# A new step table for five engines, and the output projection issued in halves instead of quarters

## The reference

```
h = exp(delta * A) * h + delta * Bm * xc        # per channel (1024) and state (16), over 8192 steps
y = sum over states of h * Cm  +  xc * D
x1 = x + ga * ((y * silu(z)) @ W_out.T)
```

## Time and profile before

| | us |
|---|---|
| median of 3 runs (5697.18 to 5701.3) | 5697.24 |
| the profiled execution, its own time | 5697.24 |
| its span, first to last instruction | 5695.4 |
| of it, chunk by chunk (from the first `times_b` of chunk 0 at 171.4 to that of chunk 15 at 3640.9), 15 chunks | 3469.5 |
| the chunk whose first `times_b` starts at 3179.88, to the next one's at 3410.47 | 230.6 |

### The profile page before, as it was taken

One profiled execution on the slowest core, in us unless ns is written; L12 is line 12 of the kernel. 1 busy time (PEld: TensorE's weight loads), 2 busy tenths in 40 slices (PEclk: granted clock), 3 DMA queues, 4 the chain that ended last, 5 costly groups with the idle time before them and its releaser, 6 DMA issues. The chain is left out here.

```text
span 5695.4 us, 76622 instructions
## 1 busy us (share of the span) xinstructions
PE 4878.5 (86%) x21894; PEld 3374.1 (59%) x21894; DVE 4986.4 (88%) x4382; ACT 3044.8 (53%) x6526; POOL 4001.5 (70%) x1946
## 2 busy tenths in 40 slices
...
GB/s 101 143 179 178 172 193 170 175 185 166 188 171 181 191 154 192 173 173 194 167 175 180 171 189 171 176 163 68 34 34 33 28 33 33 29 31 33 29 31 26
DMA packets 394604, 728.33 MB, mean 128 GB/s; under 512 B 44051, under 2 KB 44179, under 8 KB 394102
## 3 DMA queue, kind: packets, MB, share of 16 engines
...
## 5 line engine op out<-in xcount | busy, mean ns | idle before, releaser
L551 POOL TENSOR_TENSOR slot<-du,b_row 128x1024 f32<-128x1024 f32 x1024 | 2404.3, 2376 | 48.6 <-PE y_ps L914 43.8
L806 DVE TENSOR_TENSOR_SCAN decay<-decay,state,slot 128x1024 f32<-128x1024 f32 x592 | 1389.2, 2347 | 52.0 <-ACT slot L723 50.6
L714 ACT ACTIVATE decay<-delta,rate 128x512 f32<-128x512 f32 x2048 | 1326.2, 679 | 33.4 <-issue 10.6
L914 PEld LDWEIGHTS y_ps<-ident,slot 128*128 128x128 f32 x8192 | 1009.0, 150 | 334.9 <-issue 215.6
L914 PE MATMUL y_ps<-ident,slot 128*128 128x128 f32 x8192 | 1098.2, 287 | 89.0 <-POOL slot L558 83.7
L558 POOL TENSOR_TENSOR slot<-slot,c_row 128x1024 f32<-128x1024 f32 x432 | 1024.6, 2372 | 76.4 <-ACT state L703 74.0
L806 DVE TENSOR_TENSOR_SCAN slot<-decay,state,slot 128x1024 f32<-128x1024 f32 x432 | 1011.9, 2342 | 72.2 <-ACT slot L723 70.3
L1266 POOL TENSOR_TENSOR hq<-hid,qinv 128x1408 f32<-128x1408 f32 x64 | 166.4, 2600 | 1238.3 <-DVE qinv L1293 1238.3
L856 PE MATMUL work_ps<-h_t,win 128*128 128x512 f32 x2048 | 995.0, 631 | 36.0 <-DVE delta L777 19.6
L812 DVE TENSOR_TENSOR slot<-decay,c_row 128x1024 f32<-128x1024 f32 x592 | 724.3, 1224 | 56.1 <-DVE decay L806 3.2
L1234 ACT ACTIVATE act_gate<-gate_ps 128x512 f32<-128x512 f32 (+1 forms) x192 | 108.2, 564 | 1119.6 <-PE gate_ps L1375 621.5
...
## 6 DMA issues: line engine op xcount, KB each, us to landing
b_row<-b_c_rows SPq DMA_DIRECT2D x1024, 256.0 KB, 3.8
c_row<-b_c_rows SPq DMA_DIRECT2D x1024, 256.0 KB, 3.7
...
```

The lines of the kernel that those rows point to most:

```text
L551: pool.tensor_tensor(slot[:, u % SLOTS, :, :], du[:, p % 2, :, :], two(b_row[:, u % BC_RING, :]), ALU.mult).then_inc(S["ub_ready"], 1)
L714: act.activation(decay[u % 2][:, i, :], delta[:, p % 2, i, :], ACT.Exp, scale=rate[:, 2 * p + i, n:n + 1]).then_inc(S["decay_ready"], 1)
L806: dve.tensor_tensor_scan(d if u in DVE_C else h, d, h, state[:, 2 * p, n:n + 1], ALU.mult, ALU.add).then_inc(S["scan_done"], 1)
L914: op = pe.matmul(y_ps[i][:, s, :], slot[:, u % SLOTS, i, s * P:(s + 1) * P], ident[:, :], is_transpose=True, start=False, stop=(n == N - 1 ...
```

## The change

PARTS = 4 goes: a block of the output projection (8 products of 512 columns) is issued as two steps of 4 products instead of four steps of 2. All tables that say at which position a step is issued are replaced (PE, ACT, DVE, POOL, SP), and BANK is replaced. The steps themselves, their number apart from the projection's, the list DVE_C, the slots and the lags stay. Cut to its core (of ACT, DVE and SP the middle positions are left out; SP's loads and stores of the same transfers move too):

```diff
-PARTS = 4
...
 BANK = {
-    ("c", 0): 0, ("c", 1): 0, ("c", 2): 0, ("c", 3): 0, ("c", 4): 0, ("c", 5): 0, ("c", 6): 1, ("c", 7): 1,
+    ("c", 0): 0, ("c", 1): 0, ("c", 2): 0, ("c", 3): 0, ("c", 4): 0, ("c", 5): 0, ("c", 6): 0, ("c", 7): 0,
     ("d", 0): 1, ("d", 1): 1, ("d", 2): 1, ("d", 3): 1, ("d", 4): 1, ("d", 5): 1, ("d", 6): 1, ("d", 7): 1,
-    ("h", 0): 0, ("h", 1): 0, ("h", 2): 0, ("h", 3): 0, ("i", 0): 0, ("i", 1): 0, ("i", 2): 0, ("i", 3): 0,
-    ("i", 4): 0, ("i", 5): 1, ("i", 6): 1, ("i", 7): 0, ("o", 0): 0, ("o", 1): 0, ("o", 2): 1, ("o", 3): 1,
-    ("x", 0): 1, ("y", 0): 0, ("y", 1): 1, ("y", 2): 0, ("y", 3): 0, ("y", 4): 0, ("y", 5): 1, ("y", 6): 0,
-    ("y", 7): 0, ("z", 0): 0, ("z", 1): 0, ("z", 2): 0, ("z", 3): 0, ("z", 4): 0, ("z", 5): 0, ("z", 6): 1,
+    ("h", 0): 0, ("h", 1): 0, ("h", 2): 1, ("h", 3): 1, ("i", 0): 0, ("i", 1): 1, ("i", 2): 0, ("i", 3): 0,
+    ("i", 4): 1, ("i", 5): 0, ("i", 6): 1, ("i", 7): 1, ("o", 0): 0, ("o", 1): 0, ("o", 2): 0, ("o", 3): 1,
+    ("x", 0): 1, ("y", 0): 0, ("y", 1): 0, ("y", 2): 0, ("y", 3): 1, ("y", 4): 0, ("y", 5): 1, ("y", 6): 1,
+    ("y", 7): 0, ("z", 0): 1, ("z", 1): 0, ("z", 2): 0, ("z", 3): 0, ("z", 4): 0, ("z", 5): 0, ("z", 6): 0,
     ("z", 7): 0,
 }
 
 PE_STEPS = {
-    0: [("d", 3, 0), ("z", 5, 0)], 3: [("y", 6, -1)], 6: [("y", 7, -1)], 8: [("z", 6, 0)], 9: [("o", (0, 0), -1)],
-    10: [("o", (0, 1), -1)], 11: [("o", (0, 2), -1)], 12: [("o", (0, 3), -1)], 13: [("d", 4, 0)], 14: [("z", 7, 0)],
-    15: [("o", (1, 0), -1)], 16: [("o", (1, 1), -1), ("d", 5, 0)], 17: [("o", (1, 2), -1)],
-    18: [("o", (1, 3), -1), ("h", 1, 1)], 20: [("y", 0, 0), ("o", (2, 0), -1)], 21: [("o", (2, 1), -1)],
-    22: [("o", (2, 2), -1)], 23: [("o", (2, 3), -1), ("h", 3, 1)], 24: [("h", 0, 1), ("o", (3, 0), -1)],
-    25: [("o", (3, 1), -1), ("h", 2, 1)], 26: [("o", (3, 2), -1), ("i", 0, 1)], 27: [("o", (3, 3), -1), ("c", 0, 1)],
-    28: [("i", 1, 1), ("y", 1, 0)], 32: [("i", 2, 1)], 33: [("d", 6, 0)], 34: [("c", 1, 1)],
-    35: [("c", 2, 1), ("i", 3, 1), ("d", 7, 0)], 36: [("i", 4, 1)], 39: [("c", 3, 1)],
-    40: [("c", 4, 1), ("i", 5, 1), ("y", 2, 0)], 42: [("c", 5, 1), ("i", 6, 1)], 43: [("y", 3, 0)], 46: [("c", 6, 1)],
-    49: [("i", 7, 1)], 50: [("c", 7, 1)], 51: [("z", 0, 1)], 53: [("x", 0, 1)], 54: [("d", 0, 1), ("z", 1, 1)],
-    55: [("d", 1, 1)], 57: [("z", 2, 1), ("y", 4, 0)], 59: [("y", 5, 0)], 61: [("z", 3, 1)],
-    63: [("d", 2, 1), ("z", 4, 1)],
+    1: [("z", 5, 0)], 3: [("y", 6, -1)], 4: [("d", 3, 0), ("y", 7, -1)], 5: [("z", 6, 0)], 7: [("o", (0, 0), -1)],
+    8: [("o", (0, 1), -1)], 9: [("z", 7, 0), ("o", (1, 0), -1)], 10: [("o", (1, 1), -1)],
+    13: [("h", 2, 1), ("h", 3, 1)], 14: [("d", 4, 0), ("o", (2, 0), -1)], 15: [("o", (2, 1), -1)], 16: [("h", 1, 1)],
+    18: [("o", (3, 0), -1)], 19: [("o", (3, 1), -1)], 20: [("d", 5, 0)], 22: [("h", 0, 1)], 23: [("i", 0, 1)],
+    24: [("c", 0, 1)], 26: [("y", 0, 0)], 27: [("i", 1, 1)], 28: [("i", 2, 1)],
+    29: [("c", 1, 1), ("d", 6, 0), ("y", 1, 0)], 33: [("c", 2, 1)], 34: [("i", 3, 1)],
+    36: [("c", 3, 1), ("i", 4, 1), ("y", 2, 0)], 37: [("d", 7, 0)], 38: [("c", 4, 1)], 40: [("i", 5, 1)],
+    43: [("i", 6, 1)], 44: [("c", 5, 1)], 45: [("i", 7, 1)], 46: [("y", 3, 0)], 47: [("c", 6, 1)], 48: [("z", 0, 1)],
+    50: [("c", 7, 1)], 52: [("y", 4, 0)], 53: [("z", 1, 1), ("y", 5, 0)], 54: [("x", 0, 1)],
+    55: [("d", 0, 1), ("z", 2, 1)], 56: [("d", 1, 1)], 57: [("z", 3, 1)], 59: [("d", 2, 1)], 62: [("z", 4, 1)],
 }
 ACT_STEPS = {
-    0: [("sp_exp", 2, 0)], 1: [("sp_ln", 2, 0)], 3: [("z_out", 4, 0), ("xd", 0, 0)], 5: [("sp_exp", 3, 0)],
-    6: [("y_out", 6, -1), ("y_out", 7, -1)], 7: [("z_out", 5, 0)], 8: [("sp_ln", 3, 0), ("xd", 3, 0)],
-    10: [("lead", 1, 0)], 12: [("xd", 2, 0)], 13: [("z_out", 6, 0)], 14: [("seed", 0, 1)], 15: [("sp_exp", 4, 0)],
-    16: [("sp_ln", 4, 0), ("z_out", 7, 0)],
-    17: [("ln_apply", 0, 1), ("ln_apply", 1, 1), ("ln_apply", 2, 1), ("ln_apply", 3, 1)], 18: [("sp_exp", 5, 0)],
...
-    50: [("in_out", 7, 1), ("y_out", 4, 0), ("y_out", 5, 0)], 52: [("conv_out", 7, 1), ("silu_x", 0, 1)],
-    53: [("z_out", 0, 1)], 55: [("x_out", 0, 1)], 57: [("sp_exp", 0, 1), ("xd", 1, 1)], 58: [("sp_ln", 0, 1)],
-    59: [("z_out", 1, 1)], 60: [("sp_exp", 1, 1)], 61: [("sp_ln", 1, 1), ("z_out", 2, 1)], 62: [("lead", 0, 1)],
-    63: [("z_out", 3, 1)],
+    0: [("sp_exp", 2, 0)], 1: [("z_out", 4, 0)], 2: [("sp_ln", 2, 0)], 3: [("y_out", 7, -1)], 4: [("z_out", 5, 0)],
+    5: [("y_out", 6, -1)], 7: [("seed", 0, 1), ("sp_exp", 3, 0)], 8: [("ln_apply", 0, 1), ("z_out", 6, 0)],
+    10: [("ln_apply", 1, 1)], 11: [("sp_ln", 3, 0)], 12: [("z_out", 7, 0)],
+    13: [("ln_apply", 2, 1), ("ln_apply", 3, 1), ("lead", 1, 0), ("xd", 2, 0)], 14: [("h_out", 2, 1), ("h_out", 3, 1)],
+    15: [("sp_exp", 4, 0)], 17: [("sp_ln", 4, 0)], 18: [("y_out", 0, 0), ("y_out", 1, 0)], 19: [("xd", 3, 0)],
+    20: [("xd", 5, 0)], 21: [("h_out", 1, 1), ("sp_exp", 5, 0)], 22: [("h_out", 0, 1)],
...
+    49: [("conv_out", 6, 1)], 50: [("z_out", 0, 1), ("y_out", 4, 0), ("y_out", 5, 0)], 51: [("conv_out", 7, 1)],
+    52: [("silu_x", 0, 1)], 54: [("z_out", 1, 1)], 55: [("xd", 1, 1)], 56: [("x_out", 0, 1)], 57: [("sp_exp", 0, 1)],
+    58: [("sp_ln", 0, 1), ("z_out", 2, 1)], 60: [("sp_exp", 1, 1), ("xd", 0, 1)], 62: [("sp_ln", 1, 1)],
+    63: [("z_out", 3, 1), ("lead", 0, 1)],
 }
 DVE_STEPS = {
-    (0, 1): [("sp_sum", 2, 0)], (1, 1): [("sp_diff", 2, 0)], (2, 1): [("sp_out", 2, 0)], (5, 0): [("ln_stats", 0, 1)],
-    (7, 0): [("sp_sum", 3, 0)], (8, 0): [("sp_diff", 3, 0), ("gate", 6, -1)], (8, 1): [("sp_out", 3, 0)],
-    (9, 0): [("gate", 7, -1)], (10, 0): [("ln_stats", 1, 1), ("ln_stats", 2, 1), ("ln_stats", 3, 1)],
-    (10, 1): [("ln_mean", 0, 1)], (13, 1): [("residual", 0, -1)], (14, 1): [("sp_sum", 4, 0)],
-    (15, 0): [("sp_diff", 4, 0)], (16, 0): [("sp_out", 4, 0)], (18, 1): [("sp_sum", 5, 0), ("residual", 1, -1)],
-    (19, 0): [("sp_diff", 5, 0)], (19, 1): [("sp_out", 5, 0)], (21, 1): [("gate", 0, 0)],
-    (22, 0): [("residual", 2, -1)], (27, 0): [("residual", 3, -1)],
-    (27, 1): [("x1_stats", 0, -1), ("x1_stats", 2, -1)], (31, 1): [("gate", 1, 0)], (33, 1): [("sp_sum", 6, 0)],
...
-    (43, 1): [("x1_stats", 3, -1)], (46, 1): [("x1_stats", 1, -1)], (47, 0): [("gate", 3, 0)],
-    (55, 1): [("x_low", 0, 1)], (57, 1): [("sp_sum", 0, 1)], (58, 0): [("sp_diff", 0, 1)], (58, 1): [("sp_out", 0, 1)],
-    (59, 1): [("sp_sum", 1, 1)], (60, 0): [("sp_diff", 1, 1)], (60, 1): [("sp_out", 1, 1), ("gate", 4, 0)],
-    (62, 1): [("gate", 5, 0)],
+    (0, 1): [("ln_stats", 0, 1), ("ln_stats", 1, 1), ("sp_sum", 2, 0)], (3, 1): [("ln_stats", 2, 1)],
+    (4, 0): [("ln_stats", 3, 1), ("sp_diff", 2, 0)], (4, 1): [("ln_mean", 0, 1), ("sp_out", 2, 0)],
+    (5, 1): [("gate", 6, -1)], (6, 0): [("gate", 7, -1)], (9, 0): [("sp_sum", 3, 0)], (9, 1): [("residual", 0, -1)],
+    (10, 1): [("sp_diff", 3, 0)], (11, 1): [("sp_out", 3, 0)], (13, 1): [("residual", 1, -1)],
+    (15, 0): [("sp_sum", 4, 0), ("residual", 2, -1)], (16, 1): [("sp_diff", 4, 0)], (18, 0): [("sp_out", 4, 0)],
+    (20, 0): [("residual", 3, -1)], (22, 0): [("sp_sum", 5, 0)], (24, 0): [("sp_diff", 5, 0)],
+    (25, 1): [("sp_out", 5, 0), ("x1_stats", 2, -1)], (26, 1): [("gate", 0, 0)], (31, 0): [("sp_sum", 6, 0)],
...
+    (41, 1): [("sp_out", 7, 0)], (42, 1): [("x1_stats", 1, -1)], (43, 1): [("x1_stats", 3, -1)],
+    (46, 1): [("gate", 3, 0)], (51, 1): [("gate", 4, 0)], (52, 1): [("gate", 5, 0)], (56, 0): [("x_low", 0, 1)],
+    (57, 1): [("sp_sum", 0, 1)], (58, 0): [("sp_diff", 0, 1)], (58, 1): [("sp_out", 0, 1)],
+    (60, 0): [("sp_sum", 1, 1)], (61, 0): [("sp_diff", 1, 1)], (61, 1): [("sp_out", 1, 1)],
 }
 POOL_STEPS = {
-    10: [("du", 1, 0)], 15: [("lead_mul", 1, 0)], 16: [("newton", 0, 1)], 23: [("du", 2, 0)], 28: [("lead_mul", 2, 0)],
-    43: [("du", 3, 0)], 44: [("lead_mul", 3, 0)], 62: [("du", 0, 1)], 63: [("lead_mul", 0, 1)],
+    7: [("newton", 0, 1)], 13: [("du", 1, 0)], 15: [("lead_mul", 1, 0)], 28: [("du", 2, 0)], 31: [("lead_mul", 2, 0)],
+    44: [("du", 3, 0)], 47: [("lead_mul", 3, 0)], 63: [("du", 0, 1), ("lead_mul", 0, 1)],
 }
...
                     def proj_mm(arg, c):
-                        s, part = arg
+                        s, half = arg
                         b = BANK["o", s]
-                        if part == 0:
+                        if half == 0:
                             if BANK["o", s] != BANK["y", NB - 1]:
                                 wait(pe, *piece_read("y", NB - 1, c))
                             take("o", s, c)
-                        for j in range(part * NB // PARTS, (part + 1) * NB // PARTS):
+                        for j in range(half * NB // 2, (half + 1) * NB // 2):
                             op = pe.matmul(work_ps[b][:, :], xc[c.parity][:, j, s * P:(s + 1) * P], wout[:, j, :],
                                            start=(j == 0), stop=(j == NB - 1))
```

(8 more changed lines are left out.)

24 lines of the change are left out of this document (15 added, 9 removed).

## The result

| | before | after |
|---|---|---|
| median of 4 runs each, side by side (us) | 5699.04 | 5845.17 (5841.19 to 5854.15) |
| ratio, 95% interval | | 1.0256 (1.0244 to 1.0270) |
| span of the profiled execution | 5695.4 | 5843.8 |
| from the first `times_b` of chunk 0 to that of chunk 15, divided by 15 | 231.3 | 240.9 |
| the same without chunk 0, whose body has no projection, divided by 14 | 231.7 | 241.9 |

A forecast was written before the change was run, and what follows sets the result against it. POOL was taken to pace each chunk, so only its waits count: 8.0 lost early less 3.2 saved late is +4.8, taken as 4.6; 15 x 4.6 = 69 on 5697.2 gives 5766 us, 1.2% slower, range 5690 to 5820.

The forecast's parts named there:

- what paces a chunk: POOL paces a 230.6 us chunk; its operations stay, so only its 7.0 us of waits and added waits can move.
- rival "same": The two parts cancel, or POOL's work alone decides: 5697 us; chance 0.09.
- the early part's mechanism: Positions 0 to 29: late projection blocks hold DVE at residuals, so POOL waits 9.1 us instead of 1.1; 8.0 lost a chunk.
- the walk: Working the new order through one chunk, t = 0 at its first `times_b`, each step starting when engine and inputs are ready.
- the weakest step: PE's time at `z 6`, which waits for `gate 7` (27.9); 4 us there would turn the sign.
- the faster rival: Early waits are absorbed and stay at 1.1; only the late 3.2 us gain is left: 5649 us; chance 0.15.
- The step that failed first: `residual 3`, DVE position 20, reached at 83.4, waits for block 3 to 86.7; `times_c` of unit 19 waits 1.8 us.
- the late part's gain: Positions 52 to 63: POOL's waits fall from 6.0 to 2.8 us a chunk, 3.2 saved.
- The early part of before: POOL's early wait in the old kernel, taken as 1.1 us at position 6 of one chunk.
- The loop's end: The few us that every second chunk adds there were left as they are.
- The middle: Positions 30 to 51: ACT waits 1 to 2 us, but where POOL has no `times_c` soon, so 0.
- SP queue: B rows behind moved loads or stores are hidden, so no cost; without that cover up to 4.8 us a chunk.

The follow-up runs named there:

- e4: Changed kernel with 2 of the 8 products of each projection block, the other 6 left out; 5646.94 us in one run.
- e8: Changed kernel with block 3 of the projection in bank 0 at its old PE positions, h 1 behind it; 5798.36 us, ratio 1.0173.
- e1: Changed kernel with one swap, y 5 issued ahead of z 1 at PE position 53; 5819.56 us, ratio 1.0217.
- e5: Kernel before with 2 of the 8 products of each projection block, the others left out; 5675.38 us in one run.
- e9: Kernel before with d 1 moved from PE position 55 to 57, and d 3 and z 5 from 0 to 2; 5646.5 us, ratio 0.9906.
- e2: Changed kernel with block 3 in bank 0 and two PE positions earlier, ahead of h 1, residual 3 at DVE position 19; 5810.14 us, ratio 1.0200.
- e10: Changed kernel with POOL's lead_mul 0 moved from position 63 to position 0 of the next body; 5858.72 us, ratio 1.0278.

## Why the prediction was wrong in size

**Right: what paces a chunk.** POOL's work stayed at 222.9 us a chunk, and the time moved with its waits alone. The rival "same", by which POOL's work alone decides, is refuted: ranked by occupancy the engines look alike in the two kernels, and the time differs by 2.6%.

**Right: the early part's mechanism, with the walk's own numbers.** `z 6`, the weakest step, was walked to t = 27.9, and starts at 29.5 in the chunk shown (3089.28 less 3059.78). The walk had `residual 0` wait 2.2 and be served at 41.6, the trace has 2.44 and 42.8 (3102.60 less 3059.78); `residual 2` 3.9 and 68.0, the trace 3.75 and 69.7. The chunk shown begins behind the loop's pause; in bodies without it the two come at 41.9 and 68.8. POOL's waits at 12, 17 and 19 were walked as 0.9, 1.4 and 3.3 and are 1.3, 1.9 and 3.4 in the mean. That PE would be earlier and absorb them, the faster rival, did not come; e4 shows what less work of PE would have given.

**The step that failed first: `residual 3`, "reached at 83.4", waiting for block 3 "to 86.7", and POOL's 1.8 us behind it.** It was reached at 85.3 and waited to 91.5; POOL waited 4.5 in the mean. That the bank holds block 3 was in the walk ("where `d` and `xd` hold it"); that the half behind this wait runs slowly was not: its half is 3.43 us there, and took 6.57. Of the 4.8 us by which block 3 ends late, 1.7 are there already at `residual 2`, and 3.0 are the slow half. The prediction had used this very effect for `z 2` in the late part, from the row of 5.25 us after a wait, and left it out here, where it is behind a wait of 6.88 us, the second longest of PE in the chunk. This term was 2.7 us a chunk too small, of which the slow half is 2.4 by the estimate above. All early waits together (12.9 in the mean for 9.1) were 3.8 too small. e8 confirms the place: without the collision 3.1 us a chunk come back.

**The second: the late part's gain.** It was to be 6.0 to 2.8. It is 5.0 to 4.2. After: the walk put `y 5` ahead of `z 1` at PE 53 (its text does not print this step), and the table says the reverse; `gate 5` then holds DVE, and POOL waits 2.7 at 55 instead of 1.6. e1 makes that swap and gives 1.4 us a chunk. This is an error of reading, not of the chip. Before: the wait at 62 is 2.25 in the chunk that I chose and 1.4 in the mean, so one chunk was not typical there.

**An error that went the other way.** The early part of before was put at 1.1 us from one chunk. In the mean it is 2.0 (0.4 at 3, 1.6 at 6), so 0.9 us less was lost. The chunk was called typical by its sum, 7.0 for 8; its positions were not.

**The loop's end, left "as they are", cost little more than before.** The row `POOL slot <- issue` suggests otherwise: 18.9 us for 4.8, 3.6 to 4.0 each in five bodies for 0.8 to 1.1. But before, the same pause reaches POOL through ACT. In one such body (POOL, then ACT):

```profile
2018.96 2.37 POOL L551 TENSOR_TENSOR slot<-du,b_row 128x1024 f32<-128x1024 f32 x1 [1.08 <-issue]
2022.99 2.35 POOL L558 TENSOR_TENSOR slot<-slot,c_row 128x1024 f32<-128x1024 f32 x1 [1.66 <-ACT state L703]
```

```profile
2022.63 0.21 ACT L703 ACTIVATE state<-slot 128x2 f32<-128x2 f32 x1 [3.40 <-issue]
```

With that wait at the first `times_c` the pause costs POOL 1.07 us a body before and 1.35 after, over the 14 bodies. The `lead` that POOL waits 0.42 for at 63 is in the late part's 4.2, as it is in the forecast's 2.8. The ledger for a body with a projection, the forecast's 8.0 - 3.2 = 4.8 as the start:

| correction, us a chunk | |
|---|---|
| early waits after, 12.9 for 9.1 (of it 2.7 at position 21) | +3.8 |
| early waits before, 2.0 for 1.1 | -0.9 |
| late waits after, 4.2 for 2.8 | +1.4 |
| late waits before, 5.0 for 6.0 | +1.0 |
| loop's end, 1.35 after and 1.07 before, for no difference | +0.3 |
| sum with 4.8 | 10.4 |

Measured is 10.2 over these 14 bodies. Over the span, with chunk 0's 1.2 in it: 15 x 9.64 = 144.6; chunk 0's first `times_b` comes 5.0 earlier (166.4 for 171.4), a part of the start that I had taken as 0 with 5 either way; and from chunk 15's to the end it is 8.8 longer, since that chunk too has an early part with a projection (with the short projections of e4 and e5 the two kernels are alike there, 2034.2 and 2034.3). 144.6 - 5.0 + 8.8 = 148.4, the difference of the two spans. The forecast's 15 x 4.6 had the number of early parts right.

**The middle** cost nothing, as walked: POOL's waits at positions 30 to 51 come to 0.0 us a body in the mean. The **SP queue** cost nothing visible either: no row of POOL's waits names a B or C row.

**The banks of the projection.** Block 3 in a bank of its own, apart from blocks 0 to 2, was the dear one, and e8, which puts it into theirs, gained 3.1 us a chunk. The Trainium skill (Perfetto Trace Analysis, Optimizing Tensor Performance) advises rotation through the banks so that a reader overlaps the next group; in e8 the rotation is given up and the time falls. What decides here is who else uses the bank: `d 4` is held through five steps on ACT and DVE, `o 2` by one `residual`. In the shared bank 0 PE waits 0.7 us for `z_out 7` ahead of block 1, where the walk had 1.0, and 0.3 to 0.4 for `z_out 6` ahead of block 0 in half of the bodies; no run puts blocks 0 to 2 in two banks.

## What to carry to other kernels

Where every engine issues in a fixed order, price a reordering by the waits it makes on the busiest engine, not by busy time: find each long piece that waits, and look what short work stands behind it for which somebody else waits. Put a piece that must wait for another engine behind that short work; e9 gained 0.9% with two such moves, and e2 shows the reverse for a long piece. Price the piece behind a long wait of PE at what such a piece took elsewhere in the trace, not at its usual time. Read the waits by position as a mean over many bodies before summing (one chunk misled by 0.9 us in the early part and 1.0 the other way in the late part), and when a buffer is shared, ask how long the chain is that frees it.

## What the runs showed of the chip beyond what was expected

- A half of the projection took 6.57 us right behind PE's wait of 6.88, and 3.60 otherwise. The granted clock of that stretch was 0.61, a mean between the two levels of 1.2 and 2.4 GHz, and 1.00 in the crowded stretch before. PE had been busy 4.62 of the 11 us ahead of it. Over the 14 bodies the half takes 6.0 us in the mean, so this wait is paid with 6.9 us of standing and 2.4 of slow work.
- At the loop's end, in five of 14 bodies of either kernel (chunks 4, 6, 8, 10 and 12), POOL and ACT stand with nothing that the profile shows to wait for: ACT 3.0 to 3.5 us in the new kernel and 3.0 to 5.1 before, POOL 3.6 to 4.0 in the new kernel, where a wait ended right ahead of the branch, and 0.8 to 1.1 before. When `lead_mul` was taken from there (e10), POOL's was down to at most 0.7. In e8 the same pause of POOL is put down to PE's sum in four of the five bodies:

```profile
POOL slot L546 <- PE y_ps L909: 15.8, 4, 4.9
POOL slot L546 <- issue: 3.8, 1, 3.8
```

So the name "issue" is not certain, and what the engines do in the pause no view here shows.
